# Self-attention of a fused decoder layer: exp per head from the scores, then transposed

## The reference

```python
x = x + attn(layernorm(x))           # 8 heads, 2 kv heads, latent 32, causal
#   scores = einsum(q, k) * 128 ** -0.5;  scores = where(causal, scores, min)
#   y = softmax(scores) @ v;  y @ wo
x = x + xattn(layernorm(x), ctx)     # 16 heads over 77 context tokens, then
#   relu(out @ W1 + b1) @ W2 + b2
x = x + ffn(layernorm(x))            # rmsnorm, 8-bit rounding of activations,
#   ternary weights, gelu, the same again
```

## Time and profile before

| | |
|---|---|
| median of 3 runs | 319.96 us (319.79 to 321.28) |
| the profiled execution | 321.1 us, span 319.2 us |
| mean granted TensorE clock | 0.984 |
| PE busy | 302.6 us, 95% |
| DVE busy | 273.2 us, 86% |
| ACT busy | 191.0 us, 60% |
| POOL busy | 161.5 us, 51% |

### The profile page before, as it was taken

How to read it: one execution, slowest core, us unless ns; L and a number is a source line. 1 busy time by engine, 2 the same in 40 slices (tenths; PEclk the granted TensorE clock), 3 DMA queues, 4 the chain that set the end, 5 groups by cost and what they waited for, 6 DMA issues and landing times.

```text
span 319.2 us, 8883 instructions
## 1 busy us (share of the span) xinstructions
PE 302.6 (95%) x3185; PEld 248.8 (78%) x3198; DVE 273.2 (86%) x488; ACT 191.0 (60%) x369; POOL 161.5 (51%) x315
## 2 busy tenths in 40 slices
PE   8798999999999999999999999999999999998756
PEld 8476787879888887897788878887887888786534
DVE  2228996898989799999999999989999998999973
ACT  3164435436247759478966854497445965776852
POOL 7337006282933523671778266306660485077873
PEclk9899999999999999999999999999999999999978
DMA  7999000000000000000001010000000010000011
GB/s 200 340 368 330 6 3 0 2 2 0 4 2 2 3 0 2 3 0 2 2 3 34 3 35 2 2 0 4 16 18 2 2 37 2 0 3 33 3 34 66
DMA packets 11954, 12.54 MB, mean 39 GB/s; under 512 B 1668, under 2 KB 11144, under 8 KB 11912
## 3 DMA queue, kind: packets, MB, share of 16 engines
q1 hardware_dynamic: 10648, 11.40, 10.9%
q10 hardware_dynamic: 1264, 0.59, 0.7%
...
## 4 chain that ended last, share of the span: by engine, by line
PE 77%; issue 6%; DVE 6%; POOL 5%; ACT 5%; DVEq 0%; POOLq 0%; ACTq 0%
PE bank L1724 8%; PE bank L1871 7%; PE bank L1804 6%; PE bank L1894 6%; PE bank L1822 6%; PE bank L1903 5%; PE quad L1784 4%; PE bank L1885 4%; PE bank L1730 4%; PE quad L1861 3%; PE bank L1942 3%; PE bank L1757 3%; PE bank L1718 2%; PE bank L1923 2%; PE bank L1932 2%
## 5 line engine op out<-in xcount | busy, mean ns | idle before, releaser
L845 ACT ACTIVATE c_p<-bank 77x512 f32<-77x512 f32 x64 | 35.7, 591 | 26.4 <-PE bank L1871 26.2
L1871 PE MATMUL bank<-ident,c_s 128*77 128x128 f32 x256 | 34.8, 274 | 0.4 <-DVE f_o L1369 0.4
L564 POOL TENSOR_SCALAR f_s<-f_mv 128x1 f32<-128x1 f32 x16 | 3.5, 220 | 62.0 <-DVE f_s L1325 61.4
L821 ACT ACTIVATE a_p<-bank 128x512 f32<-128x512 f32 x48 | 27.3, 601 | 10.5 <-PE bank L1804 10.1
L1894 PE MATMUL bank<-c_y,xw_s 128*128 128x128 f32 x256 | 31.5, 276 | 0.8 <-DVE c_y L1303 0.8
L1871 PEld LDWEIGHTS bank<-ident,c_s 128*77 128x77 f32 x256 | 29.5, 148 | 3.1 <-issue 1.0
L1894 PEld LDWEIGHTS bank<-c_y,xw_s 128*128 128x128 f32 x256 | 30.1, 192 | 1.3 <-issue 0.9
L1903 PE MATMUL bank<-xw_s,c_h 128*128 128x256 f32 x128 | 30.5, 381 | 0.0
L1273 DVE TENSOR_REDUCE c_nm<-quad 128x16 f32<-128x1232 f32 x16 | 23.0, 1436 | 4.2 <-PE quad L1861 4.1
L1903 PEld LDWEIGHTS bank<-xw_s,c_h 128*128 128x128 f32 x128 | 23.3, 190 | 3.6 <-ACT c_h L854 0.5
L1284 DVE TENSOR_TENSOR c_s<-quad,c_nm 128x616 f32<-128x616 f32 x32 | 24.5, 792 | 1.3
...
## 6 DMA issues: line engine op xcount, KB each, us to landing
...
f_h<-in_fw1T SPq DMA_DIRECT2D x1, 1024.0 KB, 12.1
c_s<-in_fw2T SPq DMA_DIRECT2D x1, 1024.0 KB, 11.3
...
```

What stands on the lines that cost most here:

```text
L821: nc.scalar.activation(dst, src, ACT.Exp, scale=SCALE_SA).then_inc(sa.sem["act"], 1)
L845: nc.scalar.activation(c_p[0:M, :, qt * P:(qt + 1) * P].rearrange("p (c j g) t -> p c j g t", c=KC, g=Q2)[:, :, j, :, :], bank("xs", f"tr{ ...
L1871: last = nc.tensor.transpose(dst[0:M, g * P:(g + 1) * P], c_s[:, qt, j, g, :], ident[:, :])
```

## The change

ACT takes the exp straight from the quad, one instruction for each head (c, r), with the negated max as its bias column, and lets it accumulate the sum over the keys: eight instructions a unit in place of DVE's two subtractions. The score scale moves into the fold of the q weights (`pro_wqk`). The probabilities are then turned over by PE as the shifted scores were, and ACT copies them from the banks (`sa_copy`; the table `COPIED_BY` would allow DVE, and names ACT for all six). The ones half of `so_pv` goes. Instead DVE takes the reciprocals of the sums, each written 32 times (`sa_inv`, 256 elements a partition, one a unit), PE turns these over with four 128x128 transposes (`so_rd`, one bank more in the ring a batch), ACT copies that bank to `a_rd`, and DVE's `so_y` is one multiply for each c. The quad is now released by ACT's last exp of a unit. The orders of all engines and the order of the output stores are written anew; POOL's steps are the same ones.

```diff
 QUAD_EMPTIED = {
-    ("sa", "suA"): ("dve", ("sbA0", "sbA1")),
-    ("sa", "suB"): ("dve", ("sbB0", "sbB1")),
+    ("sa", "suA"): ("act", ("exA01", "exA11", "exA21", "exA31")),
+    ("sa", "suB"): ("act", ("exB01", "exB11", "exB21", "exB31")),
...
             @element
-            def sa_exp(i, u, n):
+            def sa_exp(i, u, r):
+                nm, s, w = (a_nmA, a_sA, P) if u == "A" else (a_nmB, a_sB, T)
+                qt = 0 if u == "A" else 1
+                act.wait_ge(*sa.after("dve", f"mx{u}", i))
+                act.wait_ge(*sa.after("pe", f"tr{u}{r // 2 if u == 'A' else r}", i - 1))
+                act.wait_ge(*sa.after("dve", f"inv{u}", i - 1))
+                for c in range(KC):
+                    nc.scalar.activation(s[:, r, c, :], quad[:, r, c * w:(c + 1) * w], ACT.Exp, bias=nm[:, r, c:c + 1],
+                                         accum_out=a_sum[:, qt, c, r:r + 1]).then_inc(sa.sem["act"], 1)
+
+            @element
+            def sa_copy(i, u, n):
                 act.wait_ge(*sa.after("pe", f"tr{u}{n}", i))
...
-                nc.scalar.activation(dst, src, ACT.Exp, scale=SCALE_SA).then_inc(sa.sem["act"], 1)
+                dst, src = transposed_scores(i, u, n)
+                nc.scalar.activation(dst, src, ACT.Copy).then_inc(sa.sem["act"], 1)
+
+            @element
+            def so_rd(i):
+                for c in range(KC):
+                    act.wait_ge(*so.after("dve", f"y{c}", i - 1))
+                copied(so, "so", "rd", i, flat(a_rd))
...
-            def sa_sub(i, u, e):
...
-                nc.vector.tensor_tensor(s[:, r, :, :], quad[:, r, 0:KC * w].rearrange("p r (c m) -> p r c m", c=KC),
-                                        nm[:, r, :].unsqueeze(3).to_broadcast([P, 2, KC, w]), op=ALU.add).then_inc(sa.sem["dve"], 1)
+            def sa_inv(i, u):
+                qt = 0 if u == "A" else 1
+                for r in range(4):
+                    dve.wait_ge(*sa.after("act", f"ex{u}{r}1", i))
+                dve.wait_ge(*so.after("pe", "rd", i - 1))
+                nc.vector.reciprocal(a_r[:, qt, :, :, :], a_sum[:, qt, :, :].unsqueeze(3).to_broadcast([P, KC, 4, L])).then_inc(sa.sem["dve"], 1)
...
             def so_y(i, c):
...
-                nc.vector.transpose(a_t[:, c, :, :].rearrange("p b t -> p (b t)"), src[:, T:2 * T]).then_inc(O, 1)
...
-                nc.vector.reciprocal(a_r[:, c, :], a_t[:, c, :, 0]).then_inc(O, 1)
...
-                nc.vector.transpose(a_rd[:, c, :, :], a_r[:, c, :].unsqueeze(2).to_broadcast([P, NB, 32])).then_inc(O, 1)
...
+                dve.wait_ge(*so.after("act", "rd", i))
...
             def so_pv(i, c):
...
-                for off in (0, T):
-                    for t in range(TT):
-                        for r in range(4):
-                            w = ones[:, 0:L] if off else v[:, t, group(r) * L:(group(r) + 1) * L]
...
+                for t in range(TT):
+                    for r in range(4):
+                        last = mm(dst[r * L:(r + 1) * L, t * P:T], v[:, t, group(r) * L:(group(r) + 1) * L], a_p[:, c, r, 2 * t:2 + t, :],
+                                  start=t == 0, stop=t == TT - 1)
...
+            def so_rd(i):
+                free("so", "rd", i)
+                for u in ("A", "B"):
+                    pe.wait_ge(*sa.after("dve", f"inv{u}", i))
+                for c in range(KC):
+                    for qt in range(TT):
+                        last = nc.tensor.transpose(bank("so", "rd", i)[:, c * T + qt * P:c * T + (qt + 1) * P], a_r[:, qt, c, :, :].rearrange("p r l -> p (r l)"), ident[:, :])
+                last.then_inc(so.sem["pe"], 1)
```

A stretch of the new orders of PE and of ACT, from batch 2's xs scores (xp.q) to batch 3's, as `ORDER` gives them:

```diff
 ORDER = dict(
     pe="""
...
+        xp.xT.2 xo.pv0.1 xo.pv1.1 sa.trA1.3 xp.q.2 sa.trA0.3 sa.trB2.3 xm.w10.1 xs.su0.2 sp.xT.5 f1.qT0.0 sa.trB1.3
+        xm.w11.1 sp.k.5 xs.su1.2 so.rd.3 f1.qT1.0 xm.w20.1 sa.trB0.3 xs.tr01.2 xs.tr10.2 sa.trB3.3 sa.suA.4 xs.tr11.2
+        xs.tr13.2 f1.l1_1.0 f1.l1_2.0 f1.l1_0.0 xs.tr03.2 so.pv1.3 so.pv0.3 sp.v.4 xs.tr12.2 f1.l1_3.0 sa.suB.4
+        xm.w21.1 so.wo.3 xo.pv1.2 f1.qT0.1 sp.q.5 xs.tr02.2 xs.tr00.2 sp.v.5 sa.suA.5 sa.trA0.4 sa.trA1.4 sa.trB2.4
+        xo.pv0.2 f1.l1_1.1 xm.w11.2 f1.l1_0.1 so.rd.4 f1.qT1.1 sa.suB.5 sa.trB0.4 xp.xT.3 sa.trB1.4 sa.trB3.4
+        xm.w21.2 xp.q.3 f1.l1_2.1 xm.w10.2 f1.l1_3.1 xs.su0.3 so.pv0.4 so.pv1.4 sp.xT.6 xm.w20.2 f2.hT0.0 xs.tr01.3
...
     act="""
...
+        sa.exB11.3 xp.xT.2 sa.cpA1.3 sa.exB30.3 sa.exB31.3 xp.q0.2 xp.q1.2 sa.exB00.3 sa.exB01.3 sa.cpB2.3 sa.cpA0.3
+        xm.relu00.1 xm.relu01.1 xm.relu02.1 xm.relu03.1 f1.qT0.0 sa.cpB1.3 sp.xT.5 xm.relu10.1 xm.relu11.1
+        xm.relu12.1 xm.relu13.1 sp.k.5 sp.k2.5 f2.pre.2 f1.qT1.0 so.rd.3 sa.cpB0.3 xs.ex01.2 xs.ex10.2 sa.cpB3.3
+        xs.ex11.2 xs.ex13.2 sa.exA30.4 sa.exA31.4 sa.exA10.4 sa.exA11.4 sa.exA00.4 sa.exA01.4 xs.ex03.2 sp.v.4
+        sa.exA20.4 sa.exA21.4 f1.gelu0.0 f1.gelu1.0 xs.ex12.2 sa.exB30.4 sa.exB31.4 sa.exB10.4 sa.exB11.4 sa.exB00.4
+        sa.exB01.4 sa.exB20.4 sa.exB21.4 f1.qT0.1 sp.q.5 xs.ex02.2 sp.v.5 xs.ex00.2 f2.ssq0.0 sa.cpA0.4 sa.cpA1.4
+        sa.cpB2.4 sa.exA00.5 sa.exA01.5 sa.exA20.5 sa.exA21.5 sa.exA10.5 sa.exA11.5 sa.exA30.5 sa.exA31.5 f2.pre.3
+        xm.relu10.2 xm.relu11.2 xm.relu12.2 xm.relu13.2 so.rd.4 f1.qT1.1 f2.ssq1.0 sa.cpB0.4 xp.xT.3 sa.cpB3.4
+        sa.cpB1.4 sa.exB30.5 sa.exB31.5 sa.exB10.5 sa.exB11.5 sa.exB20.5 sa.exB21.5 sa.exB00.5 sa.exB01.5 xp.q0.3
```

More of the change, by code:

```diff
@@ L1588, in _ @@
+            sa_inv(6, "B")
+            xs_max(5, 0)
+            xs_sub(5, 0, 1)
+            xs_sub(5, 0, 0)
+            xo_y(4, 0)
+            xs_max(5, 1)
+            xs_sub(5, 1, 1)
+            xs_sub(5, 1, 0)
+            sa_max(7, "A")
+            f1_h(3, 3)
+            xm_resid(4, 1)
+            f1_ln(4, 1)
+            xm_resid(4, 0)
+            so_y(6, 1)
+            so_y(6, 0)
             f1_h(3, 2)
             f2_hmax(3, 0)
-            f1_h(3, 3)
-            xs_sub(5, 0, 1)
@@ L2072, in _ @@
[L2072 to L2087 removed]
+            sp_q(4)
+            so_wo(2)
+            xs_scores(1, 1)
+            sp_v(3)
@@ new lines, in _ @@
+            f2_hT(1, 0)
+            f1_l1(2, 3)
+            f1_l1(2, 2)
+            f2_l2(0, 1)
+            xs_tr(3, 0, 2)
+            sa_tr(5, "A", 0)
+            f1_l1(2, 1)
+            sa_tr(5, "A", 1)
+            f2_hT(1, 1)
+            xs_tr(3, 1, 1)
+            xp_xT(4)
+            xo_pv(3, 0)
+            f1_l1(2, 0)
+            xs_tr(3, 1, 0)
+            xp_q(4)
+            sa_tr(5, "B", 1)
+            sa_tr(5, "B", 0)
+            sa_tr(5, "B", 2)
+            xs_scores(4, 0)
```

1867 lines of the change are left out of this document (940 added, 927 removed).

## The result

The changed kernel takes 326.42 us (median of 4 runs, 325.60 to 327.28), the kernel before beside it 320.62 us (319.79 to 321.34): ratio 1.0182, 95% interval 1.0136 to 1.0228. It is slower by 5.8 us where 6 us faster was forecast, just above the range's high end of 326.0. The profiled execution took 325.81 us with a span of 323.6.

The account below looks back on a forecast made before the run. PE was taken as the bound for three quarters of the span: 321.1 - 11.0 + 3.5 = 313.6 us, plus 2.0 of stalls 315.6 profiled, so a median of 314.5 us. Range 310.5 to 326 us.

Parts of the forecast that it names:

- earns and costs nothing: DVE's total load: falls from 273 to 248 us, less loaded than now, so no effect on the time.
- the reading of the earlier trace: From 25 to 263 us: PE, busy 236 of 238 us, sets the time; DVE keeps up at 93%, ACT has room.
- The size of the reciprocal: DVE's sa_inv: 1.38 us for each of 16 reciprocals of 256 elements, 22.1 us in all.
- The saving on PE: P·V line and so_rd: 11.0 us of ones matmuls removed, 3.5 us of transposes added, net -7.5 us.
- 2.0 us of new stalls: PE waiting on ACT in two stretches where ACT is short by 2.6 to 8.9 us: 2.0 us allowed.
- PE idle for under 5 us between 25 and 255 us: Sign that the forecast holds: PE idles less than 5 us in the middle of the span.
- The new waits: At sa_inv, ACT's so_rd copy and so_y: covered by the order, costed at nothing; uncovered, 3 to 4 us each.
- The ring rival: PE's four banks: ACT empties none during runs of eight exps, so PE stops; 327 us, chance 0.18.
- ACT's pace: Rival: ACT sets the pace in two stretches, short by 5.8 us; 318.3 us, 321.4 at the high end, chance 0.17.
- The unmoved end: Rival: the saving is made but the tail hangs on DVE, so the end stays at 320 us; chance 0.05.
- three signs of being wrong: PE waiting over 7 us on ACT's copies or exps, clock below 1.00 mid-span from stops, accumulator read costing its full 0.19 us.
- ACT's sum: ACT's busy time: 191 us plus 57 for exps, 5 for copies, less 5 for table loads, 248 us (264 high).

Follow-up runs that it names:

- e2: Changed kernel with DVE taking 8 reciprocals a unit, then writing each 32 times with a copy: 318.33 us, ratio 0.9900 to the kernel before.
- e13: Kernel before plus two 256-element DVE reciprocals a batch that nobody reads: 346.27 us, ratio 1.0781 to the kernel before.
- e1: Kernel before without the ones half of the P·V matmuls, DVE's sum steps kept: 318.16 us, ratio 0.9903 to the kernel before.
- e6: Changed kernel with reciprocals of batches 0 to 3 moved behind the next max in DVE's order at five places: 332.62 us.
- e10: Changed kernel with PE's so_rd one or two steps later each batch, ACT's copy of it later in batches 0, 2, 4: 334.30 us.
- e11: Changed kernel with 8 reciprocals a unit spread by a DVE copy, and PE's so_rd and ACT's copy of it moved later: 324.29 us.
- e3: Changed kernel with half as many exps, each over both heads of a pair with one head's max and sum: 325.81 us.
- e7: Changed kernel with the ones matmuls and DVE's old sum steps back, leaving exps, copies and new order: 332.59 us.
- e14: Kernel before without ones matmuls or DVE's sum steps, and with the max over a quarter of the score columns: 313.55 us.

## Why the prediction was wrong

**What failed: DVE "earns and costs nothing".** The step compared DVE's busy time in the new kernel with that in the old, 248 against 273 us, and concluded that less is harmless. In the new order a us of DVE costs 0.46 to 0.64 us, and the 27.4 us of spread reciprocals, in place of 8.1 for the small one and its copy, cost 9.0 us (the changed kernel against e2). The prediction costed the waits on them at nothing too; PE's waits on DVE in the stretch are 4.6 us, and none in e2. With the small form the new kernel is 3.2 us faster than before, 318.3 us and well inside the range given, so this one line of the change decides its sign.

**Behind it, the reading of the earlier trace rows.** "In three quarters of the span what PE has to stream is the time, DVE keeps up at 93%." Both numbers stand, the reading doesn't: e13 shows an added us of DVE to cost a us at that 93%. A busy share says how much an engine worked, not that the rest of its time is free. Every engine runs a fixed list, and in between it waits for what another list hands over.

**The size of the reciprocal.** 1.38 us forecast from the slope between 8 and 16 elements, 1726 ns measured: from 8 elements (203 ns) to 256 it is (1726 - 203) / 248 = 6.1 ns an element. The estimate of 2.1 us worked out from the repeat count of 8 in the Trainium skill (page "VectorE: DVE Perf Modes", section "First, the fixed hardware budget") was too high by 0.4 us, about as much as the slope was too low; the measurement decides. At 0.46 to 0.64 us for each us of DVE, the 16 x 0.35 = 5.6 us missed are by estimate some 3 of the 12 us between forecast and result. The rest would have been there at the forecast size.

**The saving on PE, taken at its full length.** -11.0 + 3.5 us went into the sum unabridged, because PE was never idle. The P·V line takes 1.44 us for its 32 records in the chain of the changed kernel, as a row had it, and four transposes 0.44 (e2's row above), as reckoned; the operations were priced well. (The list of signs says "eight transposes more"; the sum rightly has four a batch.)

```profile
227.31 1.44 PE bank L1899 x32
```

But e1 gives 3.1 us for the 11.0. The prediction allowed 2.0 us of new stalls; PE's idle time in the stretch grew by 9.2. "PE idle for under 5 us between 25 and 255 us" was named as the mark of the forecast; it is 11.3.

**The new waits, at nothing.** `so_rd`'s waits on the reciprocals are 1.7 us, and another 1.3 for the ring: small, as the text said a lost cover might be. "Without that cover each would cost about one exp run, 3 to 4 us": e6 takes it away at five places and PE waits 4.2 us at one of them, and e10 and e11 lose 6.9 us by a place alone. At that place the price was about right, and in the changed kernel most of the cover holds; that a changed place of a step costs by itself was in no term.

**The rivals.** ACT's pace as it was meant, ACT's load, is refuted: 14 us less of exps change the time by 1.1 us or nothing. ACT was reckoned well, 248 against 240.2 us busy; the exps stand 0.34 and 0.44 us apart, against 0.38 and 0.51. The ring rival named runs of eight exps as its cause. e3 speaks against that too, though it shortens each of the 16 runs by 0.9 us only. Its size came out (327 against 326.4) by luck: 9.0 us go away with the small reciprocals, which leave the runs of exps as they are. Waits through the ring exist, as e11's place at 58 to 61 us shows. The unmoved end is refuted: e1 touches nothing in the tail, and its end comes 3.1 us earlier. Of the three signs of being wrong none leads to the cause. PE's waits on ACT come to over 7 us only with the 4.4 that fall in the tail, on steps that the change doesn't touch; in the stretch they are 5.0. The accumulator's read costs 0.09 us. The granted clock did fall below 1.00 at one place, but in the faster e2 too.

**The exp part.** It went into the sum with 2.0 us of stalls for everything new on ACT; with the new order it is +11.0 us (e7), and the second half had to earn that back first. The terms of ACT's sum were right, or a little high; it was wrong to take ACT's room as the only condition.

**What stays open.** The runs don't say how much of that 11.0 belongs to the new order as such and how much to the exps standing between max and transposes. The new operations in the old order, or the reverse, weren't tried. Nor is it shown what keeps 5.5 us of PE's idle time in e14.
